# Four-direction selective scan on one NeuronCore: scans in place, and the four directions summed in DRAM

## The reference, cut to what matters

```python
delta = jax.nn.softplus(dts + dt_bias[None, :, :, None])
def step(h, inp):                       # 65536 tokens, 16 states, 256 channels
    d_t, x_t, B_t, C_t = inp
    dA = jnp.exp(d_t[..., None] * As)
    h = dA * h + (d_t * x_t)[..., None] * B_t[:, :, None, :]
    y = jnp.einsum('bkdn,bkn->bkd', h, C_t)
...
y = out_y[:, 0] + inv_y[:, 0] + wh_y + invwh_y      # the four directions, token by token
```

## Time and profile before

| | |
|---|---|
| median of three runs | 24350.81 us |
| span of the profiled execution | 24349.2 us |
| first scan to last, k = 0, 1, 2, 3 | 4975.49, 5114.55, 5086.73, 5084.39 us |
| the same for each of 128 tiles | 38.87, 39.96, 39.74, 39.72 us |
| busy over the span: PE, DVE, ACT, POOL | 96%, 96%, 93%, 85% |
| mean granted TensorE clock | 0.991 of full speed |

### The profile page before, as it was taken

The page is one execution under the profiler, slowest core; times in us unless marked ns, Lnnn a source line. Parts: engine busy times, 40 slices in busy tenths (PEclk is TensorE's granted clock), DMA queues, the critical chain, the costliest instruction groups (busy, mean ns, idle before and its releaser), DMA issues. The chain is left out here.

```text
span 24349.2 us, 520057 instructions
## 1 busy us (share of the span) xinstructions
PE 23475.9 (96%) x197068; PEld 21113.9 (87%) x197068; DVE 23408.4 (96%) x23358; ACT 22739.3 (93%) x45975; POOL 20766.4 (85%) x6924
## 2 busy tenths in 40 slices
PE   5997989999999999999999999999999999999999
PEld 2775469999999999999999899999999999999987
DVE  7998889999999999999999999999999999999996
ACT  4996579999999999999999999999999999999986
POOL 3000049999999999999999999999999999999997
PEclk8998999999999999999999999999999999999999
DMA  5222555555555555555555566666655666666665
GB/s 191 59 64 96 185 184 188 188 186 189 188 186 188 182 189 188 188 190 189 188 188 188 189 193 195 196 194 195 196 194 190 192 199 193 193 198 194 193 200 189
DMA packets 3815249, 4429.59 MB, mean 182 GB/s; under 512 B 2085381, under 2 KB 3140521, under 8 KB 3532585
## 3 DMA queue, kind: packets, MB, share of 16 engines
q1 hardware_dynamic: 3812776, 4396.31, 55.2%
HBM read 3782.68 MB, written 617.09 MB: 181 GB/s over the span
## 5 line engine op out<-in xcount | busy, mean ns | idle before, releaser
L1475 DVE TENSOR_TENSOR_SCAN s_h<-s_da,s_h,s_db 128x512 f32<-128x512 f32 x16256 | 19189.5, 1273 | 86.9 <-PE s_db L1376 86.1
L1493 POOL TENSOR_TENSOR s_prod<-s_h,s_cb 128x2048 f32<-128x2048 f32 x4096 | 18660.9, 4572 | 357.9 <-DVE s_h L1475 289.6
L1445 ACT ACTIVATE s_da<-s_delta,a_neg 128x512 f32<-128x512 f32 x16384 | 10910.5, 718 | 27.0 <-DVE s_h L1475 0.8
L1434 ACT ACTIVATE s_dxb<-s_dx,s_btok 128x256 f32<-128x256 f32 x19328 | 8592.8, 505 | 30.7 <-PEq L63 30.7
L1389 PE MATMUL s_py<-eye,s_prod 128*128 128x128 f32 x65536 | 8498.0, 273 | 15.4 <-POOL s_prod L1493 15.4
L1376 PE MATMUL s_db<-s_bdiag,s_dx 128*128 128x128 f32 x49664 | 8226.6, 275 | 0.0
L1372 PE MATMUL s_db<-eye,s_dxb 128*128 128x128 f32 x40704 | 7232.2, 275 | 309.5 <-ACT s_dxb L1434 299.9
L1389 PEld LDWEIGHTS s_py<-eye,s_prod 128*128 128x128 f32 x65536 | 7435.7, 141 | 19.4 <-POOL s_prod L1493 19.2
L1376 PEld LDWEIGHTS s_db<-s_bdiag,s_dx 128*128 128x128 f32 x49664 | 6839.4, 191 | 0.0
L1372 PEld LDWEIGHTS s_db<-eye,s_dxb 128*128 128x128 f32 x40704 | 4926.4, 141 | 1380.1 <-issue 698.3
L546 POOL COPY a_spread<-a_rden 128x256 f32<-128x256 f32 x256 | 102.8, 402 | 1645.7 <-DVE a_rden L508 1645.7
(11 more groups left out here) (141 smaller groups left out, 16291.9 us busy)
## 6 DMA issues: line engine op xcount, KB each, us to landing
s_cb<-c_rows SPq DMA_DIRECT2D x2048, 1024.0 KB, 5.8
s_bdiag<-b_diag SPq DMA_DIRECT2D x2048, 256.0 KB, 4.9
s_bdiag<-b_diag SPq DMA_DIRECT2D x1536, 192.0 KB, 6.3
y<-s_yt SPq DMA_DIRECT2D x1024, 256.0 KB, 2.7
s_xc<-xc_own SPq DMA_DIRECT2D x384, 512.0 KB, 9.4
s_yb<-y SPq DMA_DIRECT2D x768, 256.0 KB, 4.0
xc_tok<-c_ot SPq DMA_DIRECT2D x32, 2048.0 KB, 7.6
s_xt<-xc_tok SPq DMA_DIRECT2D x256, 256.0 KB, 5.2
```

What stands on the lines that cost most here:

```text
L1434: last = e.activation(dxb[:, i % NDXB, j, :], dx[:, g % 2, j, :], ACT.Copy, scale=btok[:, g % 2, 0, j, n:n + 1])
L1445: last = e.activation(da[:, i % NDA, half, :], delta[:, g % 2, half, :], ACT.Exp, scale=wts[k]["a_neg"][:, half, n:n + 1])
L1475: last = e.tensor_tensor_scan(h[:, n, half, flow], da[:, i % NDA, half, flow], db[:, i % NDB, half, flow], first, ALU.mult, ALU.add)
L1493: e.tensor_tensor(prod[:, p % GROUPS_KEPT], h[:, states], columns.unsqueeze(2).to_broadcast([P, TOGETHER, HALVES, T]), ALU.mult).then_inc( ...
```

## The change

The scan reads and writes the same array. ScalarE writes the decay straight into `h`, for all tokens but the first of the tile. For the first token VectorE itself writes decay times the last state of the tile before (`carry`, two instructions a tile, eight states each, from `fade`, two small ScalarE exponentials a tile). The scan then starts from the constant 1.0. The buffers `da` and `yb` go.

`dx` is made in every direction as it was in direction 1: TensorE turns delta, and VectorE multiplies it by the tokens `xt`, which are now loaded in every direction. GpSimd's `double` goes. Which states get three scaled pieces, and which of these GpSimd does, is a table for each direction.

There is one output tensor `y`. Direction 0 stores it as before. Directions 1 to 3 add to it in DRAM: GpSimd issues two accumulating DMAs a tile, ahead of its product 3 of the next tile. SyncE issues these stores and the loads of `yb` no more, and TensorE's adding is gone.

```diff
-    ADDED = {1: (5, 9), 2: (8, 11), 3: (8, 11)}
-    SKIPPED = 2
-    SHARE = 2
+    SKIPPED = 1
+    CARRIED = D_STATE // 2
+    CARRY_AT = {12: 0, 4: 1}
-    on_pool = lambda k, n, j: shared(k) and n % SHARE == SHARE - 1 and j == SUBS_ACT - 1
-    second_diagonal = lambda k, n: not shared(k) and n % GROUP != 0 and n != 6
-    scaled_subs = lambda k, n: SUBS_ACT - 1 if second_diagonal(k, n) else SUBS_ACT
+    WHOLE = {0: (0, 1, 4, 6, 8, 12, 15), 1: (0, 2, 4, 6, 8, 12, 15), 2: (0, 4, 8, 12), 3: (0, 4, 8, 12)}
+    POOLED = {0: (4, 8, 12), 1: (6, 12), 2: (), 3: ()}
+    SUM_AT = 3
+    on_pool = lambda k, n, j: n in POOLED[k] and j == SUBS_ACT - 1
+    scaled_subs = lambda k, n: SUBS_ACT if n in WHOLE[k] else SUBS_ACT - 1
...
-            elif stage == "dx":                                        # prepare_act
-                e.copy(flat(dx[:, s]), flat(pr[:, :, :])).then_inc(S["dx"], 1)
+            elif stage == "fade" and tile.t:
+                e.wait_ge(S["delta"], n)
+                if n >= 2:
+                    e.wait_ge(S["carry"], 2 * (n - 1))
+                for half in range(HALVES):
+                    last = e.activation(fade[:, half, :], wts[k]["a_neg"][:, half, :], ACT.Exp,
+                                        scale=delta[:, s, half, first_token(k):first_token(k) + 1])
+                last.then_inc(S["fade"], 1)
...
         PLAN_KEPT = {
             "PE": {-2: "proj0", 0: "proj1", 3: "turnb", 5: "dts", 11: "turnd"},
-            "ACT": {1: "low", 6: "exp", 7: "log", 12: "dx"},
-            "DVE": {4: "btok", 8: "delta"},
-            "POOL": {4: "double"},
+            "ACT": {1: "low", 6: "exp", 7: "log", 9: "fade"},
+            "DVE": {4: "btok", 8: "delta", 12: "dx"},
         PLAN_TURNED = {
-            "ACT": {-1: "xc", 4: "low", 8: "exp", 9: "log"},
+            "ACT": {-1: "xc", 4: "low", 8: "exp", 9: "log", 11: "fade"},
             "DVE": {6: "btok", 10: "delta", 12: "dx"},
         PLAN_BACK = {
             "PE": {2: "dts", 9: "turnd"},
-            "ACT": {3: "exp", 4: "log", 10: "dx"},
-            "DVE": {5: "delta"},
-            "POOL": {3: "double"},
+            "ACT": {3: "exp", 5: "log", 7: "fade"},
+            "DVE": {6: "delta", 10: "dx"},
...
+                        halves = slice(SKIP[place(t)[0]], SKIP[place(t)[0]] + 1) if stored(t) else slice(0, HALVES)
+                        e.dma_start(xc[:, t % 2, halves], own(*place(t))[:, halves]).then_inc(S[f"xld{t % 2}"], DMA)
                     def prefetch(g):
-                        if turned_in(place(g)[0]):
+                        if g >= 3:
+                            e.wait_ge(S["dx"], g - 2)
+                        load(e, *place(g), g % 2)
...
-                        if i >= NDA:                                   # decay
-                            scanned(e, i - NDA, HALVES - 1)
+                        if g >= 1 and n % CARRIED == 0:
+                            e.wait_ge(S["carry"], 2 * (g - 1) + n // CARRIED + 1)
-                            last = e.activation(da[:, i % NDA, half, :], delta[:, g % 2, half, :], ACT.Exp,
+                            last = e.activation(h[:, n, half, later(g)], delta[:, g % 2, half, later(g)], ACT.Exp,
...
+                    def carry(g, part):                                # vector
+                        if not 1 <= g < TILES:
+                            return
+                        states = slice(part * CARRIED, (part + 1) * CARRIED)
+                        if part == 0:
+                            e.wait_ge(S["fade"], g)
+                        multiplied(e, (g - 1) * D_STATE + (part + 1) * CARRIED - 1)
+                        e.tensor_tensor(h[:, states, :, first_token(k)], h[:, states, :, last_token],
+                                        fade[:, :, states].rearrange("p a n -> p n a"), ALU.mult).then_inc(S["carry"], 1)
-                        if g >= 1:
-                            multiplied(e, i - D_STATE)
-                            first = h[:, n, half, last_token:last_token + 1] if g else 0.0
-                            last = e.tensor_tensor_scan(h[:, n, half, flow], da[:, i % NDA, half, flow], db[:, i % NDB, half, flow],
-                                                        first, ALU.mult, ALU.add)
+                            last = e.tensor_tensor_scan(h[:, n, half, flow], h[:, n, half, flow], db[:, i % NDB, half, flow],
+                                                        1.0 if g else 0.0, ALU.mult, ALU.add)
+                        if n in CARRY_AT:
+                            carry(g if CARRY_AT[n] else g + 1, CARRY_AT[n])
...
+                    def sum_up(g):                                     # gpsimd
+                        for i in range(LINES):
+                            e.wait_ge(S[f"y{i}"], g + 1)
+                            e.dma_start(lines(y, k)[line(k, g, i)], yt[:, i * JB:(i + 1) * JB, :],
+                                        accum_op=ALU.add).then_inc(sums[g % 2], DMA)
                     for p in range(STEPS // TOGETHER):
-                        i = TOGETHER * (p + 2) + 1
-                        if shared(k) and i < STEPS:
-                            scale(i)
+                        for i in range(TOGETHER * (p + 2), min(TOGETHER * (p + 3), STEPS)):
+                            if i % D_STATE in POOLED[k]:
+                                scale(i)
+                        if k and p % (D_STATE // TOGETHER) == SUM_AT and p >= D_STATE // TOGETHER:
+                            sum_up(p // (D_STATE // TOGETHER) - 1)
                         product(p)
```

More of the change, by code:

```diff
@@ L922, in scans_phase @@
         end_block(nc, sems)
-        S = signals(sems, "load0 load1 before0 before1 store0 store1 cl0 cl1 cl2 cstore "
+        S = signals(sems, "load0 load1 store0 store1 cl0 cl1 cl2 cstore "
                           "xst0 xst1 xld0 xld1 lowld btl0 btl1 bkeep "
-                          "turned xc proj low turnb btok dts exped log delta doubled turnd dx "
-                          "scaled scaled_pool db da zero zeroed bstore bl0 bl1 bl2 bl3 h prod summed_first summed skipped added y0 y1")
+                          "turned xc proj low turnb btok dts exped log delta fade carry turnd dx "
+                          "scaled scaled_pool db da zero zeroed bstore bl0 bl1 bl2 bl3 h prod summed_first summed skipped y0 y1")
         def own(k, t):
@@ L960, in store_b @@
         def store_b(e, d, t, s):
[L962 removed]
+            for i in range(DIAGONALS):
                 there = b_diag[s, i].rearrange("(j m) -> j m", m=D_STATE * P + 1)[:, 0:D_STATE * P]
@@ L1114, in scans_phase @@
             "PE": {0: "proj0", 1: "proj1", 3: "turnb", 5: "dts", 11: "turnd"},
-            "ACT": {2: "low", 6: "exp", 7: "log", 12: "dx"},
-            "DVE": {4: "btok", 8: "delta"},
-            "POOL": {4: "double"},
+            "ACT": {2: "low", 6: "exp", 7: "log", 9: "fade"},
+            "DVE": {4: "btok", 8: "delta", 12: "dx"},
         }
@@ L1126, in scans_phase @@
             "PE": {0: "turned", 2: "proj0", 3: "proj1", 5: "turnb", 7: "dts", 11: "turnd"},
-            "ACT": {1: "xc", 4: "low", 8: "exp", 9: "log"},
+            "ACT": {1: "xc", 4: "low", 8: "exp", 9: "log", 11: "fade"},
             "DVE": {6: "btok", 10: "delta", 12: "dx"},
-            "POOL": {},
         }
@@ L1269, in _ @@
                 def _(e):
-                    def load_before(g):
-                        if g >= 1:
-                            e.wait_ge(S["added"], g)
-                        for i in range(LINES):
-                            e.dma_start(yb[:, i * JB:(i + 1) * JB, :], lines(ys[k - 1], k)[line(k, g, i)]).then_inc(S[f"before{g % 2}"], DMA)
                     def store(g):
@@ L1344, in _ @@
                                 load_low(e, *place(g + 2))
-                    store(TILES - 1)
-                    for s in range(2):
-                        e.wait_ge(S[f"store{s}"], LINES * DMA * (TILES // 2))
+                    if k == 0:
+                        store(TILES - 1)
+                    out_of(e, TILES - 2)
+                    out_of(e, TILES - 1)
                     if prepares(TILES):
@@ L1393, in total @@
                         last.then_inc(S["summed"], 1)
[L1394 to L1402 removed]
                         if n == SKIPPED and k in SKIP:
                             half = SKIP[k]
+                            if g:
+                                e.wait_ge(S[f"xld{g % 2}"], DMA * kept(g))
                             for j in range(SUBS):
@@ L1756, in build @@
     b_diag = f("b_diag", (2, 2, P * (D_STATE * P + 1)))
-    ys = [f(f"y{k}", (TOKENS, D_INNER)) for k in range(DIRECTIONS)]
+    y = f("y", (TOKENS, D_INNER))
     with ExitStack() as stack:
@@ L1760, in build @@
         sems = [stack.enter_context(nc.semaphore(f"s{i}")) for i in range(56)]
+        sums = [stack.enter_context(nc.semaphore(f"sum{i}")) for i in range(2)]
         assert all(b.num == a.num + 1 for a, b in zip(sems, sems[1:]))
```

118 lines of the change are left out of this document (46 added, 72 removed).

## The result

The changed kernel takes 26738.76 us (median of four runs, 26737.59 to 26740.91) against 24350.25 of the kernel before on the same chip: a ratio of 1.0981 [1.0965, 1.0996], 2,389 us slower. The forecast was 26,565. The span is 26739.1 us, the granted clock over it 0.961 (0.991 before).

A forecast was written before the change was run, and what follows sets the result against it. Four equally full engines were taken to bound the kernel. Tiles of 43.9, 45.2, 43.25 and 43.25 us, times 128, make 22,477 us; with 4,088 us outside the scan windows, 26,565 us, range 24,300 to 27,400.

The forecast's parts named there:

- What bounds the kernel: In the scan windows four engines are busy 97% to 99.9%, so a new wait on any is paid at once.
- The deciding term, `carry`: VectorE's two `carry` instructions a tile each wait 2.5 us for GpSimd's product in flight, 5.0 us a tile.
- The lags: GpSimd running late lengthens `carry`'s waits: 0.85 us a tile in direction 0, 2.15 in 1, 0.4 in 2 and 3.
- The step that was mis-sized, direction 1: The tile of direction 1: 38.05 of VectorE work, 5.0 of `carry` and 2.15 of lag make 45.2 us.
- The scan in place, 1.11: A VectorE scan without the pointer costs 1.11 us instead of 1.17, saving 1.9 us a tile.
- The decays' wait for `carry`: ScalarE's decays of states 0 and 8 wait for `carry`, issued four states earlier, so the wait is met.
- SyncE's work costed at nothing: SyncE's changed loads and stores stay under cover, with DMA engines at 0.57 to 0.61.
- PE and ACT at some 88%, POOL idle over 4 us a tile: Sign in the new trace: PE and ACT fall to some 88%, POOL waits over 4 us a tile for scans.
- Rival 1: `carry` does not wait, slipping between GpSimd's reads: 23,900 us, faster by 1.9%; chance 0.18.
- Rival 2: `carry` loses twice, GpSimd's next product going first: 27,430 us at half of directions 1 to 3's tiles, 28,300 at all; chance above range 0.04.
- Rival 4: `carry` does not wait, but GpSimd is bound by issuing DMAs at 2.38 us each: 24,950 us; chance 0.03.
- Rival 3: `carry` waits in part, every other one finding a gap: tile 41.2 us, about 25,100 us; chance 0.07.

The follow-up runs named there:

- Experiment 3: The kernel before, plus two VectorE multiplies of 16 columns a tile whose results nobody reads: 26958.13 us, ratio 1.107.
- experiment 1: The changed kernel with the two `carry` instructions of a tile moved from VectorE to GpSimd, behind products 5 and 7: 24145.6 us, ratio 0.9915.
- 2: The changed kernel with `carry` on VectorE as a one-element reduction reading one SBUF input, without the multiply by `fade`: 23969.72 us, ratio 0.9843.
- Experiment 4: The changed kernel with SyncE's plain stores instead of GpSimd's accumulating DMAs, leaving out the sum over directions; `carry` stays on VectorE: 26338.08 us, ratio 1.0815.
- experiment 5: The changed kernel with scans starting from a 1.0 read from SBUF by pointer instead of the constant: 27137.87 us, ratio 1.1144.
- experiment 6: The changed kernel with `carry` issued after states 3 and 11 instead of 4 and 12: 26270.42 us, ratio 1.0788.
- experiment 7: The changed kernel with `carry` on GpSimd and SyncE's plain stores instead of accumulating DMAs, leaving out the sum over directions: 23688.95 us, ratio 0.9728.

## Why the prediction was right, and where it was off

- **What bounds the kernel.** Four equally full engines, so that a wait on one is paid in full: right. Experiment 3 is the plain proof, 2,605 us for 1,016 dead multiplies.
- **The deciding term, `carry`, 2.5 us each.** Right in kind and size: the shortest medians, of the first `carry` in directions 0 and 2, are 2.55 and 2.52. That the reason is the product in flight was read before from a gate of 512 columns; for 16 columns experiment 1 shows it by taking the instruction off VectorE, 2 by changing its form alone, 3 by putting the form alone into the old kernel.
- **The lags.** 0.85 forecast in direction 0, 0.4 in 2; measured, `carry` is 5.22 and 5.27 in sum, so 0.22 and 0.27 over two bare waits. Nor do they lie where they were put. In direction 0 the first `carry` was to lag 0.75 and lags nearly nothing: `dx` stands between the second `carry` and this one, and its 1.13 us were not taken off; the same holds in direction 1, where its median is 2.66. In direction 2 the second was to take 2.5 + 0.1 and takes 2.99, by the DMAs' price below. These errors have opposite companions: VectorE idles 0.54 and 0.24 a tile, which the sum had at nothing. So the mechanism is right, but that the tiles of directions 0, 2 and 3 come out within 0.2 us is partly luck.
- **The step that was mis-sized, direction 1.** 45.2 forecast, 46.01 measured, 104 us of the 174 that were missed. Followed by its terms: scans, `btok`, `delta` and `dx` need 38.27 (38.05 forecast); `carry` 6.79 (7.15); idle 0.95 (0). The second `carry` alone was put at 2.5 + 1.4 = 3.9 and is 4.37. The DMA's price lies behind it: it was put at 1.0, and the pair takes 2.42 us, 1.21 each (the records of 1.43 overlap). With it the sum is 3.9 + 0.42 = 4.3, and in direction 2 it is 2.6 + 0.42 = 3.0. Experiment 4 takes the DMAs away, and the wait returns to 2.53. The larger part of what was missed is that VectorE now waits for PE, 0.95 us a tile, nearly all of it before the scans of states 0 and 3, behind the second `carry`. The trace of direction 1 shows how: VectorE's scans around the second `carry`,

```profile
12018.75 4.54 DVE L1466 TENSOR_TENSOR_SCAN s_h<-s_h,s_db 128x512 f32<-128x512 f32 x4
12023.21 4.35 DVE L1458 TENSOR_TENSOR s_h<-s_h,s_fade 128x16 f32<-128x16 f32 x1
```

GpSimd, whose DMAs make it late (the last two products end at 12017.56 + 9.95 = 12027.51, 9.00 us behind the scaled piece's end at 12018.51),

```profile
12011.03 2.44 POOL L1479 DMA_DIRECT2D y<-s_yt  x2
12012.57 5.49 POOL L1492 TENSOR_TENSOR s_prod<-s_h,s_cb 128x2048 f32<-128x2048 f32 x1
12017.11 1.40 POOL L1504 TENSOR_SCALAR s_dxb<-s_dx,s_btok 128x256 f32<-128x256 f32 x1
12017.56 9.95 POOL L1492 TENSOR_TENSOR s_prod<-s_h,s_cb 128x2048 f32<-128x2048 f32 x2
```

and PE, which stands 3.49 us behind the blocked scan and then runs at a lower clock, as the window below it shows (length, busy PE, PEld, DVE, ACT, POOL, clock):

```profile
12029.96 0.64 PE L1362 MATMUL s_db<-eye,s_dxb 128*128 128x128 f32 x3 [3.49 <-DVE s_h L1466]
12032.10 1.79 PE L1379 MATMUL s_py<-eye,s_prod 128*128 128x128 f32 x8
```

```profile
12025.00:12033.00 8.00, 4.51 (x29) 4.05 (x28) 8.00 (x6) 4.23 (x9) 4.45 (x2) 0.83 0.43 151
```

  The granted clock of those 8 us is 0.83, between the levels of 1.2 and 2.4 GHz, and eight transposes take 1.79 us where they take 1.04 at the full one. Over the direction it is 0.94. Such a stall of PE comes once a tile, behind the second `carry` (median 3.51 us; behind the first, 0.86). In experiment 4, with the shorter wait, the stall is 2.74 us, and VectorE idles 0.51 a tile. So "ACT and PE then have 4 to 6 us of slack" was wrong for PE behind the second wait, and right on average.
- **The scan in place, 1.11.** Right: 1.11 in every direction; experiment 5 gives the pointer's price as 1.85 us a tile against 1.9.
- **The decays' wait for `carry`.** It was said to be met, since `carry` is issued four states ahead. In directions 2 and 3 it isn't: ScalarE stands 591.3 us for it, 252 times, once in nearly every tile there. VectorE hardly pays for it, with 41.2 us of waits for ScalarE in the whole run.
- **SyncE's work costed at nothing.** Right: DMA engines at 0.55 to 0.60 as before, and no wait for a load among the large ones.
- **PE and ACT at some 88%, POOL idle over 4 us a tile.** ACT has 84%, PE 91%: its busy time rose from 23475.9 to 24204.7 us on about the same number of instructions, because of the clock: experiment 1, with the same instructions at 0.990, has 23180.1. POOL is idle (5627.15 - 4814.97) / 128 = 6.3 us a tile in direction 0, (5560.51 - 4940.60) / 128 = 4.8 in 2.
- **The rivals.** Rival 1 fell with the 2.93 us. Rival 2 did not happen where the kernel has `carry`, and did in experiment 6. Rival 4's issue-bound GpSimd is what experiment 1 has in small (tiles of 39.09 against 37.83 without DMAs). Rival 3's tile of 41.2 makes 25,180 us and not 25,100; neither came.
- **What the two expectations share that missed by most.** Experiments 5 and 6 were priced with one engine's cost changed and GpSimd's phase held still. The wait is a matter of phase: what shifts GpSimd against VectorE changes it.

Where the gain went: without `carry`'s wait the change is worth 207 us (experiment 1), and without the DMAs' share in GpSimd's time 661 (experiment 7, which leaves out the sum).

## What to carry to other kernels

Before a VectorE instruction is put beside a GpSimd stream, look at what is in flight there. What counts is how much of GpSimd's instruction is left, and a narrow instruction is no protection: 16 columns cost 2.5 us during a product of 4.56. Put such work on GpSimd itself (a median of 0.25 us here), or find a form that passes, and try it as an addition of dead work to the old kernel first, which takes one run. When a cost is the rest of somebody else's instruction, an estimate has to follow both engines' phases, and a pair of DMAs in one of them shifts everything behind it.

## What the runs showed of the hardware, unexpected

- A pair of accumulating DMAs takes 2.4 us of GpSimd's time. The two or three products behind them are recorded with about 5.5 us in place of 4.56 (row of 5.49 above), but from end to end they cost 4.5 like the others. The net price a kernel with full engines pays was 0.60 us for each DMA (experiment 7). In the changed kernel each lands in a median of 7.3 us, SyncE's plain store in 2.6.
- At 16 columns, a copy from SBUF to SBUF on VectorE waits for GpSimd's product (median 2.51 us), a reduction over one element does not (0.159).
- Whether VectorE or GpSimd goes first at a tie isn't fixed (experiment 6): 0.39 us for a `carry` at the end of a product in direction 0, 4.87 behind the DMAs in direction 2, each begun 0.35 us before a product's end.
- A scan whose start is read from SBUF by pointer costs 0.06 us more than one with a constant start, in place or not (1.17 against 1.11 for 512 columns).
